# Key lengths inverted by GpSimd's power, and unit keys formed in PSUM, in the projections of a recurrence

## The chip, the core and the metric

One core of one Trainium2 chip runs the whole program. The metric is device time in microseconds (us) of one execution, as the median of several. Of the engines, PE is TensorE, DVE is VectorE, ACT is ScalarE, POOL is GpSimd and SP is SyncE.

## The reference, cut to what matters

The program is a six-part network on x of 16 x 64 x 256. The change lies in its second part, a gated recurrence, and there in what is prepared ahead of the scan:

```python
q = jax.nn.silu(x @ Wq)
k = jax.nn.silu(x @ Wk)
v = x @ Wv
log_f = jax.nn.log_sigmoid(x @ Wf1 @ Wf2)
gamma = -jax.nn.sigmoid(x @ Wgamma)
k = l2_norm(k.reshape(b, n, H, HD))      # x / maximum(norm(x), 1e-12), 16 heads of 16
a = k * gamma[..., None] * jnp.exp(gk)   # gk is log_f, so exp(gk) = f
```

The scan of a step is S = f S; sab = a S; S = S + k (sab + v); o = q S. The kernel takes two steps at a time. For that it needs, beside k, f, v and q, the coefficient of the old state in the form of a times f, and sums over a head of q times k and of a (of the next step) times k.

## The kernel before, in words

The program is a row of stages, each a block in which the five engines run their own lists in order and wait on semaphores. The order on an engine is the order of the code. The stage of the change is `recurrence_projections_stage` (named p2, lines 234 to 564). Everything in it is float32 and lies as 128 features by 512 tokens, in two halves of the tokens (`c` is 0 or 1) and two halves of the features (`m` is 0 or 1). So nearly every elementwise instruction is 128x512.

PE makes the products in the order of the list `RJOBS` into a ring of four PSUM tiles (`acc`), each of which ACT must take before it is written again: for each c the keys k0 and k1, the low-rank input `low`, and the queries; then for each c g0, f0, g1, f1 (L461: gamma and f from 16 rows of `low`); then v0 and v1, and the output gates (L466, again from 16 rows).

The lengths of the keys go through four engines. DVE squares the activated keys (L288). PE sums the squares over each head of 16 into a corner of the PSUM tiles `n_ps` (`sums`, L474). When all four sums are there, ACT takes square roots (`lengths`, L546, four instructions of 128x32), for which it loads the table of the root, and loads that of the sigmoid again behind them. DVE bounds the lengths below, inverts them and copies each 16 times (`inverse_lengths`, L292, L294, L296, into `wide`). PE turns the copies back over features by products with the identity (`spread`, L485), into `n_ps`.

Then come the unit keys and the decay vectors. POOL squares f into `k_sig` (`decays_twice`, L393). DVE multiplies gamma by the keys (L301) and by the square of f (L304), both `fadings`. DVE multiplies the keys by the inverse length in PSUM (`units`, L308) and makes `a` from gamma and the inverse length (`decays`, L313). The DVE list is: four `inverse_lengths`; then for c = 0 two `fadings`, `units` and `decays` for each m; then the same for c = 1; then `next_decays(0)` and what follows.

Behind these stand the sums by heads. POOL multiplies even queries and odd decay vectors by the even unit keys (L398, L402), PE sums them (`by_heads`, C at L493 and A at L498), and DVE adds the results into v, a and q (L321 to L347). `by_heads(1)` overwrites the PSUM tiles of `by_heads(0)`, so its C waits for `queries(0)` on DVE (L347, semaphore q_done), whose second instruction in turn waits for POOL's `faded_queries(0)` (L410). The output gates stand last on PE. ACT takes two of them, makes 12 of the 16 first value rows (L557), once v is complete, and takes the last two gates. All engines meet at the end of the block (L280), and the recurrence begins.

Of the kernel before, what the change touches and what calls it, by code (L numbers as in the profile page):

```python
# [233 lines left out]
def recurrence_projections_stage(nc, stage, X, eps, ident, xnT, W, rows, r, low, gate, own_cols, both, first_values):  # L234
# [14 lines left out]
    with Scope(nc, stage) as sc:  # L249
# [3 lines left out]
        length, inverse = (sc.sb(n, [P, 2, KD, CH, HH]) for n in ("length", "inverse"))  # L253
# [4 lines left out]
        (acc_mm, acc_read, k_done, sq_ready, n_mm, n_taken, len_ready, inv_ready, n_ready, spread_mm, unit_ready, twice_ready, part_ready, fade_ready, a_ready, q_ready, rows_ready) = (sc.sem(n) for n in (  # L258
            "acc_mm", "acc_read", "k_done", "sq_ready", "n_mm", "n_taken", "len_ready", "inv_ready", "n_ready", "spread_mm", "unit_ready", "twice_ready", "part_ready", "fade_ready", "a_ready", "q_ready", "rows_ready"))
# [20 lines left out]
        with sc.block() as block:  # L280

            @block.vector
            def _(dve):
# [6 lines left out]
                def inverse_lengths(c, m):  # L290
                    dve.wait_ge(n_taken, ONE + KD * c + m + 1)
                    nc.vector.tensor_scalar(length[:, c, m, :, :], length[:, c, m, :, :], 1e-12, None, ALU.max).then_inc(len_ready, 1)  # L292
                    dve.wait_ge(len_ready, ONE + KD * c + m + 1)
                    nc.vector.reciprocal(inverse[:, c, m, :, :], length[:, c, m, :, :]).then_inc(inv_ready, 1)  # L294
                    dve.wait_ge(inv_ready, ONE + KD * c + m + 1)
                    nc.vector.tensor_copy(wide[:, c, m, :, :, :], inverse[:, c, m, :, :].unsqueeze(3).to_broadcast([P, CH, HH, HD])).then_inc(n_ready, 1)  # L296

                def fadings(c, m):

                    wait_read(dve, c, f"g{m}")  # L300
                    nc.vector.tensor_tensor(r["gamma"][:, m, cols(c)], r["gamma"][:, m, cols(c)], r["k"][:, m, cols(c)], ALU.mult).then_inc(part_ready, 1)  # L301
                    dve.wait_ge(part_ready, ONE + KD * c + m + 1)
                    dve.wait_ge(twice_ready, ONE + KD * c + m + 1)
                    nc.vector.tensor_tensor(r["gamma"][:, m, cols(c)], r["gamma"][:, m, cols(c)], r["k_sig"][:, m, cols(c)], ALU.mult).then_inc(fade_ready, 1)  # L304

                def units(c, m):
                    dve.wait_ge(spread_mm, ONE + KD * c + m + 1)
                    nc.vector.tensor_tensor(r["k"][:, m, cols(c)], r["k"][:, m, cols(c)], n_ps[m][:, :], ALU.mult).then_inc(unit_ready, 1)  # L308

                def decays(c, m):  # L310
                    dve.wait_ge(fade_ready, ONE + KD * c + m + 1)
                    dve.wait_ge(spread_mm, ONE + KD * c + m + 1)
                    nc.vector.scalar_tensor_tensor(r["a"][:, m, cols(c)], r["gamma"][:, m, cols(c)], -1.0, n_ps[m][:, :], ALU.mult, ALU.mult).then_inc(a_ready, 1)  # L313

                def next_values(c):

                    dve.wait_ge(A_mm, ONE + c + 1)
                    dve.wait_ge(a_ready, ONE + 2 * KD)
                    for m in range(KD):
                        wait_read(dve, c, f"v{m}")  # L320
                    nc.vector.tensor_tensor(xv_ps, A_ps, steps("v", c, 0), ALU.mult).then_inc(xv_ready, 1)  # L321
                    dve.wait_ge(xv_ready, ONE + c + 1)
                    nc.vector.tensor_tensor(steps("v", c, 1), xv_ps, steps("v", c, 1), ALU.add).then_inc(v_done, 1)

                def next_decays(c):

                    dve.wait_ge(A_mm, ONE + c + 1)
                    dve.wait_ge(a_ready, ONE + 2 * KD)
                    nc.vector.tensor_tensor(xa_ps, A_ps, steps("a", c, 0), ALU.mult).then_inc(xa_ready, 1)
# [30 lines left out]
                for c in range(2):  # L360
                    for m in range(KD):
                        squares(c, m)
                for c in range(2):
                    for m in range(KD):
                        inverse_lengths(c, m)
                for c in range(2):
                    for m in range(KD):
                        fadings(c, m)
# [16 lines left out]
            def _(pool):  # L385
# [4 lines left out]
                def decays_twice(c, m):  # L390
                    pool.wait_ge(k_done, ONE + KD * c + m + 1)
                    wait_read(pool, c, f"f{m}")
                    nc.gpsimd.tensor_tensor(r["k_sig"][:, m, cols(c)], r["f"][:, m, cols(c)], r["f"][:, m, cols(c)], ALU.mult).then_inc(twice_ready, 1)  # L393
# [27 lines left out]

                for c in range(2):
                    for m in range(KD):
                        activated(c, m)
                for c in range(2):
                    for m in range(KD):
                        decays_twice(c, m)
                for c in range(2):
                    faded_twice(c)
# [7 lines left out]
                faded_queries(1)  # L437
                for c in range(2):
                    faded_keys(c)

            @block.tensor
            def _(pe):
# [34 lines left out]
                def spread(c, m):  # L477

                    pe.wait_ge(n_ready, ONE + KD * c + m + 1)
                    pe.wait_ge(n_taken, ONE + 2 * KD)  # L480
# [32 lines left out]
                for m in range(KD):  # L513
                    spread(0, m)
# [13 lines left out]
            def _(act):  # L528
# [15 lines left out]
                def lengths(c, m):  # L544
                    act.wait_ge(n_mm, ONE + 2 * KD)
                    nc.scalar.activation(length[:, c, m, :, :], n_ps[m][:, CH * HH * c:CH * HH * (c + 1)].rearrange("p (j h) -> p j h", j=CH), ACT.Sqrt).then_inc(n_taken, 1)  # L546
# [6 lines left out]
                for c, name in RJOBS:  # L553
# [7 lines left out]
                    if (c, name) == (1, "q1"):  # L561
                        for half in range(2):
                            lengths(half, 0)
                            lengths(half, 1)
# [2477 lines left out]
```

## Time and profile before

| what | value |
|---|---|
| median of 3 runs | 907.91 us (907.48 to 908.52) |
| profiled execution, first to last instruction (its span) | 905.5 us |
| what lies around the span, by the median | 2.4 us |
| PE / DVE / ACT / POOL busy | 85% / 63% / 48% / 34% |
| the stage's part that the change touches | from 199.6 to 238.7 us |

The profiled execution's own time is not given apart from its span, so the median less the span stands for what lies around it. Busy shares are averages over the whole span; in a stage of this kind another engine ends the waits. In a timeline a group of instructions is one line, with the start of the first and the time to the end of the last. Instructions of one engine overlap a little, so distances between starts are shorter than durations.

### The profile page before, as it was taken

The page shows a single profiled execution, that of the slowest core. Times are in us where ns is not written, and L with a number is a line of the kernel's source. Part 1 is how long each engine was busy: PE and PEld are TensorE (multiplying, and loading weights), DVE is VectorE, ACT ScalarE, POOL GpSimd, SP SyncE. Part 2 cuts the span into 40 slices and gives each one's busy share as a digit, 9 for nine tenths or more (in the row PEclk, how much of TensorE's full clock was granted, in tenths as well). Part 3 has the DMA queues.
Part 4 walks back from the last instruction along what each step waited for, and adds up shares of the span by engine and source line. Part 5 has one row for each costly group of instructions (what it writes and reads, how often), then busy time and mean ns, then how long its engine had stood idle before and what let it go on. Part 6 is the DMA issues. An engine that isn't in the chain of part 4 may idle for free. (4 is left out here: it accounts for less than half of the span.)

```text
span 905.5 us, 19140 instructions
## 1 busy us (share of the span) xinstructions
PE 767.5 (85%) x7000; PEld 514.0 (57%) x7000; DVE 569.9 (63%) x1297; ACT 431.1 (48%) x1284; POOL 312.1 (34%) x374
## 2 busy tenths in 40 slices
PE   5999999698899999968777399999289886867997
PEld 4788888445433333355456288887167774465334
DVE  3555555539699999977796533322587776455474
ACT  3656666462474664235365100000368883655572
POOL 2111120027477888721450441100643432233001
PEclk9899999897699999988897599999588997989899
DMA  7012530000020000000001046632545310000001
GB/s 259 18 43 52 190 107 1 2 1 1 23 71 0 1 1 1 0 1 0 2 2 48 24 149 199 186 105 82 179 146 177 107 50 2 1 3 3 0 1 49
DMA packets 44893, 51.79 MB, mean 57 GB/s; under 512 B 7072, under 2 KB 40832, under 8 KB 44544
## 3 DMA queue, kind: packets, MB, share of 16 engines
q1 hardware_dynamic: 40256, 43.48, 15.3%
q0 software_dynamic: 1536, 4.20, 1.5%
q10 hardware_dynamic: 3008, 2.88, 0.9%
q8 instruction: 57, 0.93, 0.4%
q14 instruction: 36, 0.29, 0.1%
HBM read 45.31 MB, written 5.24 MB: 56 GB/s over the span
## 5 line engine op out<-in xcount | busy, mean ns | idle before, releaser
L968 PE MATMUL r_u_ps<-r_t_in,l_same_head 128*128 128x512 f32 x124 | 69.5, 643 | 1.0
L1362 ACT ACTIVATE a_prob<-a_s_ps,a_negmax 128x256 f32<-128x256 f32 x128 | 59.1, 486 | 19.8 <-DVE a_negmax L1418 19.8
L936 POOL TENSOR_TENSOR r_q_in<-r_state,rec_q 128x512 f32<-128x512 f32 x62 | 68.0, 1097 | 0.0
L1705 ACT ACTIVATE a_prob<-a_s_ps,a_negmax 128x256 f32<-128x256 f32 x128 | 58.6, 484 | 19.3 <-DVE a_negmax L1743 19.2
L2275 PE MATMUL m_h_ps<-m_rowsT,l_w 128*128 128x256 f32 x256 | 58.8, 391 | 0.0
L1424 DVE COPY a_probT<-a_w_ps 128x512 f32<-128x512 f32 x48 | 31.5, 687 | 38.9 <-PE a_w_ps L1283 38.6
L1743 DVE TENSOR_REDUCE a_negmax<-a_s_ps 128x2 f32<-128x512 f32 x64 | 40.9, 682 | 23.0 <-PE a_s_ps L1632 23.0
L2275 PEld LDWEIGHTS m_h_ps<-m_rowsT,l_w 128*128 128x128 f32 x256 | 50.4, 197 | 7.2
L2286 PE MATMUL m_y_ps<-l_w,m_hidden 128*128 128x256 f32 x240 | 53.9, 379 | 0.0
L2321 ACT ACTIVATE m_rowsT<-m_xt_ps,l_B_s,l_B_g 128x256 f32<-128x256 f32 x16 | 8.2, 560 | 93.2 <-PE m_xt_ps L2263 93.2
L2189 DVE TENSOR_SCALAR m_hidden<-m_h_ps,l_b 128x256 f32<-128x256 f32 x64 | 28.0, 479 | 37.9 <-PE m_h_ps L2275 37.9
L926 POOL TENSOR_TENSOR r_faded<-r_state,rec_both 128x256 f32<-128x256 f32 x62 | 39.8, 641 | 33.4 <-DVE r_state L905 33.4
L1418 DVE TENSOR_REDUCE a_negmax<-a_s_ps 128x2 f32<-128x512 f32 x64 | 39.7, 683 | 17.9 <-PE a_s_ps L1274 17.9
L2286 PEld LDWEIGHTS m_y_ps<-l_w,m_hidden 128*128 128x128 f32 x240 | 45.2, 190 | 5.8
L1202 POOL TENSOR_TENSOR a_spread<-a_rden,all_half 128x256 f32<-128x256 f32 x16 | 9.8, 614 | 106.6 <-DVE a_rden L1430 106.6
L1641 PE MATMUL a_w_ps<-all_ident,a_prob 128*128 128x128 f32 x256 | 39.5, 299 | 8.3 <-ACT a_prob L1705 7.2
L896 DVE TENSOR_TENSOR r_update<-r_u_ps,rec_k 128x512 f32<-128x512 f32 x64 | 44.3, 693 | 1.6 <-PE r_u_ps L962 1.5
L892 DVE TENSOR_TENSOR r_t_in<-r_state,r_par_ps 128x512 f32<-128x512 f32 x62 | 42.6, 687 | 3.2
L1942 POOL TENSOR_TENSOR a_prob<-a_prob,a_rden 128x512 f32<-128x512 f32 x32 | 32.3, 1042 | 33.6 <-DVE a_rden L2008 33.6
L2213 POOL DMA_INDIRECT m_rows<-routed_rows,m_token x16 | 15.4, 964 | 79.8 <-PE m_xt_ps L2263 43.6
L1641 PEld LDWEIGHTS a_w_ps<-all_ident,a_prob 128*128 128x128 f32 x256 | 31.2, 154 | 17.7 <-issue 9.4
L1232 PE MATMUL a_w_ps<-a_ctxT,l_A_WkT 128*128 128x256 f32 x128 | 33.1, 404 | 7.1 <-DMA l_A_WkT<-in_A_WkT 5.9
(377 smaller groups left out, 1893.1 us busy)
## 6 DMA issues: line engine op xcount, KB each, us to landing
l_w<-in_B_w SPq DMA_DIRECT2D x16, 1024.0 KB, 5.7
a_ctxT<-in_ctxT SPq DMA_DIRECT2D x31, 256.0 KB, 2.9
a_ctx<-in_ctx SPq DMA_DIRECT2D x16, 256.0 KB, 2.8
expert_out<-m_y ACTq DMA_DIRECT2D x7, 256.0 KB, 5.6
all_X<-in_x SPq DMA_DIRECT2D x4, 256.0 KB, 5.3
l_b<-in_B_b SPq DMA_DIRECT2D x1, 1024.0 KB, 5.2
all_xnT<-own_rows SPq DMA_DIRECT2D x1, 1024.0 KB, 5.4
routed_rows<-ffn_xn SPq DMA_DIRECT2D x8, 128.0 KB, 1.8
```

Of the source, the lines that this page charges most:

```text
L892: nc.vector.tensor_tensor(t_in[m][:, :, :, :], twice(state[n % 2][m]), a, ALU.mult).then_inc(t_ready[m], 1)
L896: nc.vector.tensor_tensor(update[m][:, :, :, :], u_ps[m][:, :, :, :], steps("k", 2 * n, 2, m), ALU.mult).then_inc(upd_ready[m], 1)
L926: nc.gpsimd.tensor_tensor(faded[m][:, :, :], state[n % 2][m][:, :, :], f, ALU.mult).then_inc(faded_ready[m], 1)
L936: ins = nc.gpsimd.tensor_tensor(q_in[i % 2][m][:, :, :, :], twice(state[i % 2][m]), steps("q", 2 * i - 1, 2, m), ALU.mult)
L968: nc.tensor.matmul(u_ps[m][:, :, :, :], same_head[:, :], t_in[m][:, :, :, :], start=False, stop=True).then_inc(u_mm[m], 1)
L1362: ins = nc.scalar.activation(prob[n % 2][:, r, m, :], s_ps[r][:, m, :], ACT.Exp, bias=negmax[n % 2][:, r, m:m + 1], accum_out=den[n % 2][: ...
L1418: nc.vector.tensor_reduce(negmax[n % 2][:, r, :], s_ps[r][:, :, :], AX.X, ALU.max, negate=True).then_inc(max_ready, 1)
L1641: mm = nc.tensor.transpose(acc[:, (2 * m + c) * P:(2 * m + c + 1) * P], prob[n % 2][:, r, m, c * P:(c + 1) * P], ident[:, :])
L1705: ins = nc.scalar.activation(prob[n % 2][:, r, m, :], s_ps[r][:, m, :], ACT.Exp, bias=negmax[n % 2][:, r, m:m + 1], accum_out=den[n % 2][: ...
L1743: nc.vector.tensor_reduce(negmax[n % 2][:, r, :], s_ps[r][:, :, :], AX.X, ALU.max, negate=True).then_inc(max_ready, 1)
L2275: mm = nc.tensor.matmul(h_ps[i][:, f, :], w1[j][:, k, (2 * i + f) * P:(2 * i + f + 1) * P], rowsT[j][:, k, :], start=(k == 0), stop=(k == ...
L2286: mm = nc.tensor.matmul(y_bank(e, slice(c, c + 1))[:, 0, :], hidden[j][:, f, c * P:(c + 1) * P], w2[j][:, f, :], start=(f == 0), stop=(f = ...
```

## The change

It has six parts, all in this stage.

1. DVE bounds the sums of squares (by 1e-24) straight out of PSUM (`lengths`, two instructions of 128x64), and POOL raises them to the power -0.5 (`inverse_lengths`, two instructions of 128x64 against a tile of -0.5). ACT's four roots, DVE's four clamps of 128x32 and four reciprocals are gone. POOL does the powers between its third and its fourth activation of q.
2. ACT squares f (`decays_twice`), between its sigmoids.
3. POOL multiplies gamma by the square of f (`fadings`); the multiplication of gamma by the keys is gone.
4. DVE writes the unit keys over the inverse lengths in PSUM (`units`), makes `a` from them and gamma (`decays`), and ACT copies the unit keys to SBUF (`take_units`): c = 0 behind its last f, c = 1 behind v1 of c = 0.
5. PE spreads c = 0 between the g and f products of c = 0 and those of c = 1, before behind both.
6. POOL makes `both` (f even times f odd) behind the faded queries, before ahead of the first query sums.

```diff
+                def lengths(m):
+                    dve.wait_ge(n_mm, ONE + KD * 2)
+                    nc.vector.tensor_scalar(length[:, m, :, :, :], n_ps[m][:, 0:2 * CH * HH].rearrange("p (c j h) -> p c j h", c=2, j=CH), 1e-24, None, ALU.max).then_inc(n_taken, 1)
+                def spread_lengths(c, m):
+                    dve.wait_ge(inv_ready, ONE + m + 1)
+                    nc.vector.tensor_copy(wide[:, c, m, :, :, :], inverse[:, m, c, :, :].unsqueeze(3).to_broadcast([P, CH, HH, HD])).then_inc(n_ready, 1)
                 def units(c, m):
                     dve.wait_ge(spread_mm, ONE + KD * c + m + 1)
-                    nc.vector.tensor_tensor(r["k"][:, m, cols(c)], r["k"][:, m, cols(c)], n_ps[m][:, :], ALU.mult).then_inc(unit_ready, 1)
+                    nc.vector.tensor_tensor(n_ps[m][:, :], n_ps[m][:, :], r["k"][:, m, cols(c)], ALU.mult).then_inc(unit_mul, 1)
                 def decays(c, m):
+                    dve.wait_ge(unit_mul, ONE + KD * c + m + 1)
                     dve.wait_ge(fade_ready, ONE + KD * c + m + 1)
-                    nc.vector.scalar_tensor_tensor(r["a"][:, m, cols(c)], r["gamma"][:, m, cols(c)], -1.0, n_ps[m][:, :], ALU.mult, ALU.mult).then_inc(a_ready, 1)
+                    nc.vector.scalar_tensor_tensor(r["a"][:, m, cols(c)], n_ps[m][:, :], -1.0, r["gamma"][:, m, cols(c)], ALU.mult, ALU.mult).then_inc(a_ready, 1)
...
+                def inverse_lengths(m):
+                    pool.wait_ge(exponent_ready, ONE + 1)
+                    pool.wait_ge(n_taken, ONE + m + 1)
+                    nc.gpsimd.tensor_tensor(inverse[:, m, :, :, :], length[:, m, :, :, :], minus_half[:, :, :, :], ALU.pow).then_inc(inv_ready, 1)
+                def fadings(c, m):
+                    wait_read(pool, c, f"g{m}")
+                    pool.wait_ge(twice_ready, ONE + KD * c + m + 1)
+                    nc.gpsimd.tensor_tensor(r["gamma"][:, m, cols(c)], r["gamma"][:, m, cols(c)], r["k_sig"][:, m, cols(c)], ALU.mult).then_inc(fade_ready, 1)
...
+                def decays_twice(c, m):
+                    act.wait_ge(k_done, ONE + KD * c + m + 1)
+                    wait_read(act, c, f"f{m}")
+                    nc.scalar.activation(r["k_sig"][:, m, cols(c)], r["f"][:, m, cols(c)], ACT.Square).then_inc(twice_ready, 1)
+                def take_units(c, m):
+                    act.wait_ge(a_ready, ONE + KD * c + m + 1)
+                    nc.scalar.activation(r["k"][:, m, cols(c)], n_ps[m][:, :], ACT.Copy).then_inc(unit_ready, 1)
```

`next_values` and `next_decays` on DVE write over `n_ps` and so wait, beside what they waited for, for all four copies of the unit keys.

The rows below are the order of instructions on an engine, with no times. POOL in this stage, before (`rec_` are the tensors of the recurrence, `p_` those of the stage, `rec_k_sig` holds the square of f):

```order
L388 TENSOR_TENSOR rec_q<-rec_q,rec_q_sig 128x512 x4
L393 TENSOR_TENSOR rec_k_sig<-rec_f 128x512 x4
L420 TENSOR_TENSOR rec_both<-rec_f 128x2x256 x2
L398 TENSOR_TENSOR p_q_with_k<-rec_q,rec_k 128x512
L402 TENSOR_TENSOR p_a_with_k<-rec_a,rec_k 128x512
L406 TENSOR_TENSOR rec_a<-rec_a,rec_f 128x2x256
```

And with the change:

```order
L426 MEMSET p_minus_half 128x64
L385 TENSOR_TENSOR rec_q<-rec_q,rec_q_sig 128x512 x3
L391 TENSOR_TENSOR p_inverse<-p_length,p_minus_half 128x64 x2
L385 TENSOR_TENSOR rec_q<-rec_q,rec_q_sig 128x512
L397 TENSOR_TENSOR rec_gamma<-rec_gamma,rec_k_sig 128x512 x4
L402 TENSOR_TENSOR p_q_with_k<-rec_q,rec_k 128x512
L406 TENSOR_TENSOR p_a_with_k<-rec_a,rec_k 128x512
L410 TENSOR_TENSOR rec_a<-rec_a,rec_f 128x2x256
```

The two powers stand ahead of the fourth activation, and the four products with gamma ahead of the first product of q and k.

PE from the last sum of squares to the first sums by heads, before:

```order
L474 MATMUL p_n_ps<-l_head_of,rec_a 128x8 x4
L461 MATMUL p_acc<-rec_low,l_R_up 128x512 x8
L485 MATMUL p_n_ps<-all_ident,p_wide 128x128 x8
L454 MATMUL p_acc<-all_xnT,l_R_Wv 128x512 x2
L485 MATMUL p_n_ps<-all_ident,p_wide 128x128 x8
L454 MATMUL p_acc<-all_xnT,l_R_Wv 128x512 x2
L493 MATMUL p_x_turned<-p_q_with_k,l_same_head 128x512
```

And with the change:

```order
L482 MATMUL p_n_ps<-l_head_of,rec_a 128x8 x4
L469 MATMUL p_acc<-rec_low,l_R_up 128x512 x4
L493 MATMUL p_n_ps<-all_ident,p_wide 128x128 x8
L469 MATMUL p_acc<-rec_low,l_R_up 128x512 x4
L462 MATMUL p_acc<-all_xnT,l_R_Wv 128x512 x2
L493 MATMUL p_n_ps<-all_ident,p_wide 128x128 x8
L462 MATMUL p_acc<-all_xnT,l_R_Wv 128x512 x2
L501 MATMUL p_x_turned<-p_q_with_k,l_same_head 128x512
```

The first spread has moved ahead of the second four g and f products, which now queue behind it.

## Rows read from the trace of the kernel before

**Rows 1.** The page: granted clock of PE in 40 slices of the span.

```profile
PEclk9899999897699999988897599999588997989899
```

**Rows 2.** Windows: stretch and length in us, busy us of each engine, clock, DMA.

```profile
199.60:238.70 39.10, 31.52 (x89) 18.40 (x89) 29.77 (x46) 15.80 (x35) 23.66 (x17) 0.72 0.00 1
203.80:213.50 9.70, 9.70 (x27) 6.78 (x28) 9.53 (x14) 3.57 (x7) 7.74 (x7) 0.50 0.00 0
229.50:236.70 7.20, 7.20 (x17) 5.15 (x16) 5.50 (x11) 3.97 (x12) 1.95 (x2) 0.50 0.00 0
```

**Rows 3.** Timeline of ACT: start, us, instruction, idle before.

```profile
200.06 1.28 ACT L546 ACT_TABLE_LOAD   x1
201.83 1.28 ACT L538 ACT_TABLE_LOAD   x1
203.12 0.60 ACT L538 ACTIVATE rec_gamma<-p_acc 128x512 f32<-128x512 f32 x1
...
233.82 3.71 ACT L557 ACTIVATE all_QT<-rec_v,l_diag 128x128 f32<-128x128 f32 x12
237.34 1.09 ACT L541 ACTIVATE rec_gate<-p_acc 128x512 f32<-128x512 f32 x2
```

**Rows 4.** Timeline of PE, 199 to 237 us.

```profile
199.63 1.99 PE L461 MATMUL p_acc<-rec_low,l_R_up 16*128 16x512 f32 x8
203.77 4.27 PE L461 MATMUL p_acc<-rec_low,l_R_up 16*128 16x512 f32 x8 [2.15 <-ACT rec_gamma L538]
207.97 3.78 PE L485 MATMUL p_n_ps<-all_ident,p_wide 128*128 128x128 f32 x16
211.54 2.99 PE L454 MATMUL p_acc<-all_xnT,l_R_Wv 128*128 128x512 f32 x4
214.37 1.95 PE L485 MATMUL p_n_ps<-all_ident,p_wide 128*128 128x128 f32 x16
216.15 1.88 PE L454 MATMUL p_acc<-all_xnT,l_R_Wv 128*128 128x512 f32 x4
217.87 1.02 PE L493 MATMUL p_x_turned<-p_q_with_k,l_same_head 128*128 128x512 f32 x2
218.73 1.02 PE L498 MATMUL p_x_turned<-p_a_with_k,l_same_head 128*128 128x512 f32 x2
219.59 3.60 PE L454 MATMUL p_acc<-all_xnT,l_R_Wv 128*128 128x512 f32 x8
226.62 1.26 PE L493 MATMUL p_x_turned<-p_q_with_k,l_same_head 128*128 128x512 f32 x2 [3.43 <-DVE rec_q L347]
229.51 7.19 PE L466 MATMUL p_acc<-l_R_up,rec_low 16*128 16x256 f32 x16
```

**Rows 5.** Timeline of DVE.

```profile
202.18 0.43 DVE L296 COPY p_wide<-p_inverse 128x512 f32<-128x512 f32 x1
...
205.85 0.82 DVE L296 COPY p_wide<-p_inverse 128x512 f32<-128x512 f32 x1
...
214.78 1.88 DVE L304 TENSOR_TENSOR rec_gamma<-rec_gamma,rec_k_sig 128x512 f32<-128x512 f32 x1
...
221.78 0.70 DVE L329 TENSOR_TENSOR p_n_ps<-p_x_turned,rec_a 128x512 f32<-128x512 f32 x1
...
225.78 0.69 DVE L347 TENSOR_TENSOR rec_q<-p_x_turned,rec_q 128x512 f32<-128x512 f32 x1
```

**Rows 6.** Groups by line, POOL and DVE: busy us, mean ns, idle before.

```profile
L936 POOL TENSOR_TENSOR r_q_in<-r_state,rec_q 128x512 f32<-128x512 f32 x62 | 68.0, 1097 | 0.0
L926 POOL TENSOR_TENSOR r_faded<-r_state,rec_both 128x256 f32<-128x256 f32 x62 | 39.8, 641 | 33.4 <-DVE r_state L905 33.4
L388 POOL TENSOR_TENSOR rec_q<-rec_q,rec_q_sig 128x512 f32<-128x512 f32 x4 | 5.1, 1265 | 30.6 <-ACT rec_q_sig L538 30.6
L398 POOL TENSOR_TENSOR p_q_with_k<-rec_q,rec_k 128x512 f32<-128x512 f32 x2 | 3.0, 1504 | 3.3 <-DVE rec_k L308 3.2
...
L304 DVE TENSOR_TENSOR rec_gamma<-rec_gamma,rec_k_sig 128x512 f32<-128x512 f32 x4 | 5.4, 1347 | 0.1
```

More of the change, by code:

```diff
@@ L252, in recurrence_projections_stage @@
         n_ps = [sc.ps(f"n_ps{j}", [P, N]) for j in range(KD)]
-        length, inverse = (sc.sb(n, [P, 2, KD, CH, HH]) for n in ("length", "inverse"))
+        length, inverse = (sc.sb(n, [P, KD, 2, CH, HH]) for n in ("length", "inverse"))
+        minus_half = sc.sb("minus_half", [P, 2, CH, HH])
         wide = sc.sb("wide", [P, 2, KD, CH, HH, HD])
@@ L288, in squares @@
                     nc.vector.tensor_tensor(r["a"][:, m, cols(c)], r["k"][:, m, cols(c)], r["k"][:, m, cols(c)], ALU.mult).then_inc(sq_ready, 1)
[L290 to L304, printed above, removed]
+                def lengths(m):
+                    dve.wait_ge(n_mm, ONE + KD * 2)
+                    nc.vector.tensor_scalar(length[:, m, :, :, :], n_ps[m][:, 0:2 * CH * HH].rearrange("p (c j h) -> p c j h", c=2, j=CH), 1e-24, None, ALU.max).then_inc(n_taken, 1)
@@ L362, in _ @@
                         squares(c, m)
+                for m in range(KD):
+                    lengths(m)
                 for c in range(2):
                     for m in range(KD):
-                        inverse_lengths(c, m)
+                        spread_lengths(c, m)
                 for c in range(2):
-                    for m in range(KD):
-                        fadings(c, m)
                     for m in range(KD):
@@ L420, in faded_twice @@
                     nc.gpsimd.tensor_tensor(both[:, :, c * N // 2:(c + 1) * N // 2], steps("f", c, 0), steps("f", c, 1), ALU.mult).then_inc(both_faded, 1)
+                nc.gpsimd.memset(minus_half[:, :, :, :], -0.5).then_inc(exponent_ready, 1)
+                activated(0, 0)
+                activated(0, 1)
+                activated(1, 0)
+                for m in range(KD):
+                    inverse_lengths(m)
+                activated(1, 1)
                 for c in range(2):
                     for m in range(KD):
[L424 to L429, printed above, removed]
+                        fadings(c, m)
                 queries_with_keys(0)
@@ L437, in _ @@
                 faded_queries(1)
+                for c in range(2):
+                    faded_twice(c)
                 for c in range(2):
@@ L512, in _ @@
                         product(c, name)
-                for m in range(KD):
-                    spread(0, m)
+                    if c == 0:
+                        for m in range(KD):
+                            spread(0, m)
                 product(0, "v0")
@@ L560, in _ @@
                         normed.take(act, 4 + ("k0", "k1", "low", "q0").index(name))
[L561 to L564, printed above, removed]
+                    if name == "g1":
+                        decays_twice(c, 0)
+                    if name == "f1":
+                        decays_twice(c, 1)
+                    if (c, name) == (1, "f1"):
+                        take_units(0, 0)
+                        take_units(0, 1)
+                    if (c, name) == (0, "v1"):
+                        take_units(1, 0)
+                        take_units(1, 1)
 def gated_output_stage(nc, stage, history, own, ident, gate, gated, gain, Wo, X, eps):
```

16 lines of the change are left out of this document (5 added, 11 removed).

## The prediction, blind

> **What bounds the kernel now.** I read the page first. PE is busy for most of the span, but that is an average over stages, and its clock dips in single slices [rows 1]. So I read the stage of the change by itself. Of its 39.1 us from the first g product to the start of the recurrence, PE shows 31.5 us busy at a mean granted clock of 0.72 [rows 2]: neither PE nor any other engine is full. DMA moves nothing. What ends the stage has to be followed wait by wait.
>
> From the end backwards: ACT ends last, at 238.4 us, with two gates of 1.09 us behind twelve value rows of 3.71 us [rows 3]. These waited for the second gate from PE, whose four gate products begin at 229.51 and take 7.19 us at half clock [rows 2, 4]. Ahead of them PE stood idle for 3.43 us, up to 226.62, for DVE's `queries(0)` (L347), which ended at 226.47 [rows 4, 5]. PE had offered the sums for DVE's chain of seven instructions (L329 to L347) at 219.6, but DVE reached the first only at 221.78 [rows 4, 5]. DVE was late for two reasons. Its inversion began only after ACT's table load of 1.28 us [rows 3], and its eight `fadings` instructions run slowly: L304 takes 1.35 us on average and up to 1.88, where L329, which has one operand in PSUM, takes 0.70 [rows 5, 6]. Both operands of L304 lie in SBUF, where POOL is at work at the same time, so I put it down to the two engines waiting for each other there.
>
> The front of the stage has its own stall: ACT is held by two table loads with the roots between them from 200.06 to 203.12 [rows 3], PE's ring is full, PE is idle for 2.15 us, and from 203.77 it runs at half clock, the lower of its two levels (1.2 against 2.4 GHz), for 9.7 us [rows 2, 4].
>
> **The change, part by part.** All times are those of the profiled execution, whose span is 905.5 us; the median is 2.4 us above the span, and I move both by the same amount.
>
> *ACT's front.* The two table loads and the roots go: 203.12 less 200.06 is 3.1 us, which ACT gets back [rows 3]. It gets four squares and four copies of 128x512, at 0.55 us each (two gates in 1.09) 4.4 us in all. ACT is busy 15.8 of 39.1 us [rows 2, 3], so this is covered; only the place of a copy matters, below.
>
> *The powers.* The last sum of squares is there at about 199.6 [rows 4], DVE's two clamps of 64 columns take an estimated 0.2 us each (a copy of 512 takes 0.43 [rows 5]), and POOL's first power starts near 200.0 and the second behind it. No row shows a power on POOL. Let X be its time for 128x64. From below: POOL's product costs 0.641 us for 256 columns and 1.097 for 512 [rows 6], so 1.78 ns a column, and 64 columns cost 0.3 us. From above, a power is a chain of arithmetic on each column (a logarithm, a product, an exponential). I choose its length: 12 passes at 1.78 ns give 64 x 12 x 1.78 = 1.4, with 0.2 us of start about X = 1.6 to 1.7; 40 passes give 4.8 us, my upper bound. I take **X = 1.7**, which is nearer to the row of the product, the one operation of this form that the trace has, than to the upper bound, and I keep 0.3 and 4.8 for the range.
>
> *DVE's copies.* A copy into `wide` takes 0.43 us alone and 0.82 beside POOL [rows 5]: it was held until POOL's instruction ended. So I let the first copy start not at the end of the first power but at the end of the second, 200.0 + 2 X = 203.4, and the first spread can start at 203.85. If the copy could run beside the power instead, the first spread would start at about 202.2 and the sum would be up to 1.6 us better; the row speaks against that.
>
> *PE's middle.* From 201.5 to 203.85 PE is idle, as long as before, so I keep half clock behind it. Then: two spreads 3.6, the second four g and f products 3.8 (between twice their full-clock time, 3.4, and the 4.2 of before), v0 2.8, two spreads 1.8, v1 1.7, the two sums by heads 1.7 [rows 4]. That ends at 219.3. Before, it was 219.6. The gain of 3.1 us at the front is thus nearly all spent on the powers and the idle time ahead of the spread. Moving the spread ahead costs nothing, since g and f for c = 1 are wanted later.
>
> *DVE and POOL behind it.* DVE loses its 8 `fadings` instructions, the slow ones, and the reciprocals. The four products with gamma go to POOL, at 1.27 us each [rows 6], and end near 213, before `a` of c = 1 is wanted. The copies of the unit keys for c = 1 stand on ACT behind v1 of c = 0: PE ends v1 at 217.7, ACT takes it by 218.3, and the two copies behind it end near 219.3. So DVE starts its chain when PE's sums are there, at 219.5 and not 221.78: **2.3 us** earlier. Its last instruction waits for POOL's `faded_queries(0)`: three POOL products of 1.50 us [rows 6] behind the last unit key give 219.3 + 4.5 = 223.8. The chain would have been ready at 223.5. So `queries(0)` ends at 224.6, and **1.9 us** are left of the 2.3. `both`, moved behind these, has cover: POOL ends near 230 to 232, ahead of ACT.
>
> *The last stretch.* PE's wait before the second sums shrinks from 3.43 us to about 1.9. In before, the clock fell in these sums, and the gates ran at half: the sums took 2.9 us (226.62 to 229.51) and the first two gates 3.5 of the 7.19. At full clock the same work takes 1.7 and 1.7 us (L493 and L498 start 0.86 us apart there [rows 4]), 3.0 less. Before, a stall of 2.15 us was followed by half clock, and one of 3.43 too; 1.9 us has no row. I take 2.3 of the 3.0. Behind the second gate, 3.6 for value rows and 1.1 for gates remain as they are.
>
> **Sum:** -1.9 - 2.3 = **-4.2 us**, that is 907.9 - 4.2 = 903.7 us. The end moves by about 2 us for each us of X, since both powers stand ahead of the first copy.
>
> **The rivals.** *A. The power is nearly as cheap as a product (X of 0.3 to 0.8).* Then the first spread starts 2 to 2.8 us earlier, PE's idle time is under 1 us, and part of the 3.9 us that half clock costs in spreads and g and f products goes too. At X = 0.3: -4.2 - 2.8 - 2.4 = -9.4, so 898.5 us. For it: the memory side of 64 columns is tiny. Against: a power is no single pass.
>
> *B. The power takes what it frees (X near 4).* At X = 3.8 the sum is -4.2 + 2 x 2.1 = 0, about 908 us. ACT's 3.1 us then only became POOL's wait. For it: each step of the chain may wait for the one before. No row of before shows such a chain.
>
> *C. Slower: POOL becomes the bound of the stage.* The mechanism is one: the power, at the head of POOL's in-order list, holds the fourth activation, the four products with gamma and all that DVE and PE do behind it. It decides from X = 4.7 on, where the sum passes +1.8. At X = 6, +8.6 - 4.2 = +4.4, or 912 us. A first call that has to fetch code would do the same: once Y us ahead of the first power move the end by Y, and above 6 us they make it slower. The Trainium skill (GPSIMD Engine Reference, section Instruction dispatch) states a load of about 6 us for the first call of a freshly loaded function; with that the sum would be +1.8. Against it: on POOL's list no instruction is added besides the product form with another operation.
>
> *D. The clock stays low in the last stretch.* Then only -1.9 us, 906.0 us. It lies inside the forecast's own range.
>
> **How the numbers follow.** About 0.2% (1.8 us) is what a measurement of this kernel can tell from no change. The forecast (X from 0.8 to 2.9, with D in it) has a chance of 0.44 and 901 to 906 us; A 0.20; B (X of 2.9 to 4.7) 0.18; C 0.18. Faster by over 0.2% is the forecast and A: 0.64. The range takes in X = 0.3 at the low end (898.5) and X = 4.8 at the high end (-4.2 + 6.2 = +2.0, so 910): it leaves out C but for its edge.
>
> **What would show it.** In the profile after: no table load between 199 and 204 us; two powers on POOL with their length X, right behind 200.0; the first copy into `wide` starting or ending only behind the second power; PE idle from 201.5 to about 203.9; L329's like on DVE (now L326) at 219.5 with the wait ended by PE or ACT, not by DVE's own work; `queries(0)` ended by POOL's faded queries; ACT's last gate at 234.2 against 238.4. Wrong would be: X over 3 us; PE at full clock through the first spreads (better than said); a `take_units` copy or a POOL product with gamma on which DVE waits for over 1 us beyond this schedule; or a recurrence stage whose own length differs by more than 1 us.

## The result, and the profile after

The change makes the kernel slower: 923.91 us (923.09 to 924.91) against 908.21 us, a ratio of 1.0172 with a 95% interval of 1.0156 to 1.0188. The forecast was 903.7 us, and the range ended at 910.0. The loss is 15.7 us.

The whole of it lies in the stage of the change. From the first product of g to the first product of the recurrence, before took 238.74 - 199.63 = 39.1 us [rows 2, 4], the second time by this line:

```profile
238.74 5.46 PE L962 MATMUL r_u_ps<-all_QT,l_same_head 128*128 128x512 f32 x6 [2.04 <-PEq L280]
```

After, by PE's timeline (start, us, instruction, idle before and what ended it):

```profile
199.04 1.99 PE L469 MATMUL p_acc<-rec_low,l_R_up 16*128 16x512 f32 x8
210.75 2.08 PE L493 MATMUL p_n_ps<-all_ident,p_wide 128*128 128x128 f32 x8 [9.72 <-DVE p_wide L298]
222.21 2.08 PE L493 MATMUL p_n_ps<-all_ident,p_wide 128*128 128x128 f32 x8 [9.38 <-DVE p_wide L298]
224.21 3.79 PE L469 MATMUL p_acc<-rec_low,l_R_up 16*128 16x512 f32 x8
...
236.77 1.02 PE L506 MATMUL p_x_turned<-p_a_with_k,l_same_head 128*128 128x512 f32 x2
...
243.21 1.64 PE L501 MATMUL p_x_turned<-p_q_with_k,l_same_head 128*128 128x512 f32 x2 [1.98 <-DVE rec_q L344]
...
254.19 4.35 PE L982 MATMUL r_u_ps<-all_QT,l_same_head 128*128 128x512 f32 x6 [3.73 <-PEq L281]
```

It is 254.19 - 199.04 = 55.2 us, 16.0 more. PE has no table load to wait for, and still stands idle for 9.72 and 9.38 us ahead of the two first spreads; in before it had one wait of 2.15 us here, ahead of the second g and f products [rows 4]. Each time it waits for a copy into `wide` on DVE. DVE in turn waits for POOL (its lines stand in the last section), whose timeline is this:

```profile
199.52 21.12 POOL L391 TENSOR_TENSOR p_inverse<-p_length,p_minus_half 128x64 f32<-128x64 f32 x2 [1.35 <-DVE p_length L294]
220.61 1.25 POOL L385 TENSOR_TENSOR rec_q<-rec_q,rec_q_sig 128x512 f32<-128x512 f32 x1
```

Two powers of 64 columns fill 21.1 us, 10.57 each. The view of the tile `p_inverse` gives the shortest, the median and the longest in nanoseconds:

```profile
L391 POOL TENSOR_TENSOR p_inverse<-p_length,p_minus_half x2: 10544/10566/10589, 199.5 to 210.1; 128x64 f32<-128x64 f32 x2
```

I had taken 1.7 us for each, and 4.8 us as the upper bound. Behind the powers the order of the waits is the foreseen one, with a lower clock than I had. From the second of the two spreads (222.21) to the recurrence it takes 32.0 us. The forecast had 30.7 us (203.85 to 238.74 - 4.2), with both spreads in them. v0 and the spreads of c = 1 took 3.78 and 2.85 us, at a granted clock of 0.53 from 222.2 to 234.0, and I had written 2.8 and 1.8.

### The profile page after: what moved, and what is told of

Read it like the earlier page. It is cut to its first block and busy times, and to the rows that moved or that the text cites. A ratio compares the mean times of both kernels' runs of the same rounds, so it can differ in the third digit from the quotient of the medians.

```text
span 921.5 us, 19133 instructions
## 1 busy us (share of the span) xinstructions
PE 765.9 (83%) x7000; PEld 511.0 (55%) x7000; DVE 560.5 (61%) x1283; ACT 433.1 (47%) x1286; POOL 333.3 (36%) x377
## 5 line engine op out<-in xcount | busy, mean ns | idle before, releaser
L1382 ACT ACTIVATE a_prob<-a_s_ps,a_negmax 128x256 f32<-128x256 f32 x128 | 59.2, 486 | 19.5 <-DVE a_negmax L1438 19.5
```

The source lines that it names most:

```text
L1382: ins = nc.scalar.activation(prob[n % 2][:, r, m, :], s_ps[r][:, m, :], ACT.Exp, bias=negmax[n % 2][:, r, m:m + 1], accum_out=den[n % 2][: ...
```

## The experiments

Twelve kernels ran. Three of them leave the inverse lengths out and are there for their time alone: `exponent_one`, `product` and `product_x16`. The stage's length is taken from one profiled execution each, from the first g product to the first product of the recurrence; the ratio is that of the whole program, against executions of before made beside it.

| run | stage, us | less before | ratio, 95% interval |
|---|---|---|---|
| before | 39.1 | | |
| the change | 55.2 | +16.0 | 1.0172 (1.0156 to 1.0188) |
| product | 31.8 | -7.3 | 0.9915 (0.9890 to 0.9941) |
| product_x16 | 35.3 | -3.8 | 0.9951 (0.9931 to 0.9971) |
| quarters | 49.0 | +9.9 | one execution |
| exponent_one | 55.3 | +16.2 | one execution |
| power_alone | 60.0 | +20.9 | 1.0253 (1.0228 to 1.0278) |
| roots | 35.1 | -4.0 | 0.9967 (0.9948 to 0.9985) |
| fadings_dve | 35.4 | -3.7 | 0.9954 (0.9931 to 0.9977) |
| old_units | 36.1 | -3.0 | 0.9979 (0.9956 to 1.0002) |
| reordered | 33.5 | -5.6 | 0.9925 (0.9902 to 0.9947) |
| newton3 | 35.8 | -3.3 | 0.9945 (0.9920 to 0.9969) |
| newton2 | 37.1 | -2.0 | 0.9966 (0.9938 to 0.9994) |
| gates_early | 36.3 | -2.8 | 0.9985 (0.9957 to 1.0013) |

Before itself spread over 906 to 914 us in these executions, so differences of 2 us in the whole program are at the edge of what they tell. Part of the spread comes from elsewhere. Behind the first product of the recurrence the profiled execution took 666.1 to 667.7 us in ten of the fourteen kernels, before and the change among them, and 670.0 to 670.8 us in `quarters`, `power_alone`, `roots` and `old_units`. In three of the four the difference comes up some 430 us later, in an attention stage that none of the edits touches, and in `power_alone` mostly in a later one; why is not known. So the stage and the whole can differ by 3 to 4 us for one kernel.

### What a power costs

**Fewer columns in each power.** Four powers of 128x32, in the order of the halves c.

```diff
-                    nc.gpsimd.tensor_tensor(inverse[:, m, :, :, :], length[:, m, :, :, :], minus_half[:, :, :, :], ALU.pow).then_inc(inv_ready, 1)
+                    nc.gpsimd.tensor_tensor(inverse[:, m, c, :, :], length[:, m, c, :, :], minus_half[:, c, :, :], ALU.pow).then_inc(inv_ready, 1)
```

> The change with four powers of 128x32 in place of two of 128x64. If a power's time goes by its columns (165 ns each): 5.3 us each, and the last copy starts at the same time as in the change; time within 2 us of it. If it is a fixed time for each instruction (code fetched or a call set up anew each time): 10.5 us each, 42 us in all, and some 20 us longer.

The view of the tile, in nanoseconds (shortest, median, longest):

```profile
L391 POOL TENSOR_TENSOR p_inverse<-p_length,p_minus_half x4: 5416/5419/5467, 200.5 to 216.8; 128x32 f32<-128x32 f32 x4
```

5.42 us for 32 columns and 10.57 for 64: (10.57 - 5.42) / 32 = 0.161 us a column, and 0.27 us beside them, which is what a product of this size costs in all. So the time goes by columns. The stage was 6.1 us shorter than the change's, which I had not expected: both halves m of c = 0 are inverted after 11 us and not after 21. It was not more, since DVE's list has the unit keys behind the fourth copy, and PE then waited 5.13 us for ACT's copies of them. The one time measured was 921.73 us, 2.2 us below the change. The stage also began 1.0 us later in this execution, and what lies behind it took 670.7 us against 667.3, so of the 6.1 us 1.7 are left in the span.

**Other data.** An exponent of 1.0.

```diff
-                nc.gpsimd.memset(minus_half[:, :, :, :], -0.5).then_inc(exponent_ready, 1)
+                nc.gpsimd.memset(minus_half[:, :, :, :], 1.0).then_inc(exponent_ready, 1)
```

> The change with 1.0 in place of -0.5 as the exponent, so that the lengths are not inverted. If the time of a power goes by its data (a general path for roots, a short one for whole numbers): well under 10.5 us each. If not: 10.5 us each and the time of the change, 924 us.

```profile
L391 POOL TENSOR_TENSOR p_inverse<-p_length,p_minus_half x2: 10544/10567/10590, 200.3 to 210.8; 128x64 f32<-128x64 f32 x2
```

The same to a nanosecond, and 924.43 us. No short path for an easy exponent shows.

**No power, its place kept short.** A product stands in the place of each power.

```diff
-                    nc.gpsimd.tensor_tensor(inverse[:, m, :, :, :], length[:, m, :, :, :], minus_half[:, :, :, :], ALU.pow).then_inc(inv_ready, 1)
+                    nc.gpsimd.tensor_tensor(inverse[:, m, :, :, :], length[:, m, :, :, :], minus_half[:, :, :, :], ALU.mult).then_inc(inv_ready, 1)
```

> The change with both powers replaced by products of the same shape (128x64), so that the inverse lengths are left out and the unit keys are wrong by a factor. Theory 1 (the time of the power on POOL is the whole loss, and the rest of the change gains what the blind sum gave it at X = 0.3): 898.5 us, 9.4 below before. Theory 2 (the end moves by 2 us for each us of X from the measured end of the change, since both powers stand ahead of nearly everything): 923.9 - 2 x (10.57 - 0.3) = 903.4 us, 4.5 below before. Theory 3 (the other five parts cost about what they free): 907 to 909 us.

901.43 us, 7.2 below before (908.67). That lies between theories 1 and 2 and rules out the third: all that is not the powers is a gain, taken together. PE's timeline has three lines for the rest:

```profile
202.68 2.07 PE L493 MATMUL p_n_ps<-all_ident,p_wide 128*128 128x128 f32 x16
...
220.74 1.10 PE L501 MATMUL p_x_turned<-p_q_with_k,l_same_head 128*128 128x512 f32 x2 [1.98 <-DVE rec_q L344]
...
223.38 7.19 PE L474 MATMUL p_acc<-l_R_up,rec_low 16*128 16x256 f32 x16
```

PE goes without idle time into the first spread, which now runs at full clock (2.07 us for 16, against 3.78 [rows 4]). But the wait ahead of the second sums is still 1.98 us, and the gates behind it take 7.19 us, as in before. That is nearly all that my -9.4 had too much: up to the second sums the run is 7.0 us ahead of before (220.74 - 200.77 against 226.62 - 199.63), where the sum for X = 0.3 had 1.9 + 2.8 + 2.4 = 7.1. The last stretch then gave 0.3 us, and I had taken 2.3.

**The power's place held for 1.6 us.**

```diff
+                    pool.wait_ge(q_ready, ONE + 1)
+                    nc.gpsimd.tensor_tensor(both[:, m, :], r["q"][:, 0, 0:N], r["q_sig"][:, 0, 0:N], ALU.mult)
+                    nc.gpsimd.tensor_tensor(inverse[:, m, :, :, :], length[:, m, :, :, :], minus_half[:, :, :, :], ALU.mult).then_inc(inv_ready, 1)
```

> The change with each power replaced by two products, one of 128x512 (1.27 us) into a tile that is written later anyway and one of 128x64 (0.3 us), so that the place of the power is held for some 1.6 us and the inverse lengths are left out. Theory 1 (my blind sum was right but for X, and 2 us go with each us of X): 903.7 us by the blind sum, 901.4 + 2 x 1.3 = 904.0 us from the run with products. Rival (below some length the powers lie beside ACT's first sigmoids and cost nothing, since PE's queue has other work): 901 to 902 us.

904.88 us against 909.19, a ratio of 0.9951, so 4.5 us less (3.8 in the stage). The blind sum with an X of this size was -4.2. So the sum held for its X, but two errors in it nearly cancel, which is luck. Up to the second sums the run is 1.0 us ahead of before (225.62 - 199.67 against 226.62 - 199.63), and I had 1.9; behind them it gains 2.8 more, and I had 2.3. The first copy did not wait for the second stand-in. It started beside that one's product of 128x512 and took 1.48 us, and PE idled 1.59 and 0.53 us and not 2.3:

```profile
201.71 1.48 DVE L298 COPY p_wide<-p_inverse 128x512 f32<-128x512 f32 x1 [1.57 <-POOL p_inverse L393]
203.40 4.30 DVE L298 COPY p_wide<-p_inverse 128x512 f32<-128x512 f32 x3 [0.21 <-POOL p_inverse L393]
```

Between this run and the change X differs by 9.0 us and the stage by 19.9, so the end moves by 2.2 us for each us of X. I had said about 2.

**The powers alone in the kernel before.** Parts 2 to 6 of the change are undone.

```diff
-                        activated(c, m)
+                nc.gpsimd.memset(minus_half[:, :, :, :], -0.5).then_inc(len_ready, 1)
+                activated(0, 0)
+                activated(0, 1)
+                activated(1, 0)
+                for m in range(KD):
+                    powers(m)
+                activated(1, 1)
```

> The kernel before with part 1 of the change alone (clamps out of PSUM on DVE, powers on POOL, no roots and no reciprocals). Theory 1: 21.1 us of powers against 3.1 us of roots and loads on ACT; DVE's fadings and POOL's squares of f stand behind the powers, so 908.7 + 18 = 926 to 928 us, 2 to 4 above the change. Rival (the other parts cost something that the power hides in the change): below 923 us.

931.63 us, a ratio of 1.0253: worse than I expected and 7.7 us above the change. 4.9 us of that lie in the stage (60.0 against 55.2), and 2.7 behind it, where the edits do not reach (670.0 against 667.3). POOL's and DVE's timelines show what comes behind the powers:

```profile
222.19 5.02 POOL L401 TENSOR_TENSOR rec_k_sig<-rec_f 128x512 f32<-128x512 f32 x4
227.17 2.93 POOL L428 TENSOR_TENSOR rec_both<-rec_f 128x512 f32<-128x512 f32 x2
```

```profile
226.34 1.41 DVE L305 TENSOR_TENSOR rec_gamma<-rec_gamma,rec_k_sig 128x512 f32<-128x512 f32 x1
...
234.66 1.87 DVE L305 TENSOR_TENSOR rec_gamma<-rec_gamma,rec_k_sig 128x512 f32<-128x512 f32 x1
236.46 1.98 DVE L302 TENSOR_TENSOR rec_gamma<-rec_gamma,rec_k 128x512 f32<-128x512 f32 x1
```

The squares of f queue behind the powers on POOL, and then run beside DVE's slow products. So parts 2 to 6 are worth 4.9 us of the stage behind the powers. With roots they are worth 4.0 (next run); from one execution each, the two can't be told apart with certainty.

### What the other parts are worth

**Roots on ACT again.** The change with ACT's roots and DVE's clamps and reciprocals in place of the powers.

```diff
-                    nc.gpsimd.tensor_tensor(inverse[:, m, :, :, :], length[:, m, :, :, :], minus_half[:, :, :, :], ALU.pow).then_inc(inv_ready, 1)
+                    nc.scalar.activation(length[:, m, :, :, :], n_ps[m][:, 0:2 * CH * HH].rearrange("p (c j h) -> p c j h", c=2, j=CH), ACT.Sqrt).then_inc(n_taken, 1)
...
+                    nc.vector.tensor_scalar(length[:, m, :, :, :], length[:, m, :, :, :], 1e-12, None, ALU.max).then_inc(len_ready, 1)
+                    nc.vector.reciprocal(inverse[:, m, :, :, :], length[:, m, :, :, :]).then_inc(inv_ready, 1)
```

> The change without the powers: ACT takes square roots (two of 128x64, two table loads around them) and DVE clamps and inverts (two of each), as before, with the other five parts of the change as they are. Theory 1 (the power alone is the loss; fadings off DVE and the unit keys in PSUM gain): the unit chain on DVE starts about 2 us earlier than before, 903 to 905 us. Theory 3 (the other parts gain nothing): 907 to 909 us.

906.01 us, a ratio of 0.9967 (0.9948 to 0.9985): faster than before, by 3.0 us in the ratio (1.4 to 4.7) and 4.0 in the stage. The stage's gain lies in the 3.7 to 5.7 that I expected, the whole a little below them. The chain on DVE behind the first sums by heads starts 18.0 us behind the first g product (218.90, from the line below, less 200.92), and not 22.2 (221.78 - 199.63, [rows 4, 5]). Its start now waits for PE and no longer for DVE's own work, as the blind text said:

```profile
218.90 0.70 DVE L326 TENSOR_TENSOR p_n_ps<-p_x_turned,rec_a 128x512 f32<-128x512 f32 x1 [1.57 <-PE p_x_turned L497]
...
223.44 0.69 DVE L344 TENSOR_TENSOR rec_q<-p_x_turned,rec_q 128x512 f32<-128x512 f32 x1 [0.58 <-POOL rec_q L408]
```

**The products with gamma on DVE.** In the run with roots, `fadings` moves from POOL to DVE, ahead of the unit keys of each half.

```diff
-                    nc.gpsimd.tensor_tensor(r["gamma"][:, m, cols(c)], r["gamma"][:, m, cols(c)], r["k_sig"][:, m, cols(c)], ALU.mult).then_inc(fade_ready, 1)
+                    nc.vector.tensor_tensor(r["gamma"][:, m, cols(c)], r["gamma"][:, m, cols(c)], r["k_sig"][:, m, cols(c)], ALU.mult).then_inc(fade_ready, 1)
```

> The run with roots, with the four products of gamma and the square of f back on DVE, ahead of the unit keys of each half. If it was POOL's taking them that gains: DVE's instructions beside POOL take 1.4 to 1.9 us again and come ahead of the decay vectors; 1 to 2 us above the run with roots (906.0). If it was leaving out the other product (gamma times the keys) and the order: the same as the run with roots.

904.28 us, a ratio of 0.9954, and 35.4 us in the stage against 35.1; the intervals of the two ratios overlap for the most part. In this schedule POOL is idle while DVE multiplies, and the four instructions take 0.69 us each. So it isn't POOL's taking them that gains.

**Parts 2, 5 and 6 alone.** The kernel before with squares of f on ACT, the first spread early and `both` late; unit keys, roots and all eight products of DVE stay.

```diff
-                    nc.gpsimd.tensor_tensor(r["k_sig"][:, m, cols(c)], r["f"][:, m, cols(c)], r["f"][:, m, cols(c)], ALU.mult).then_inc(twice_ready, 1)
+                    nc.scalar.activation(r["k_sig"][:, m, cols(c)], r["f"][:, m, cols(c)], ACT.Square).then_inc(twice_ready, 1)
```

> The kernel before with parts 2, 5 and 6 of the change alone: ACT squares f, the first spread stands ahead of the second g and f products, both is made late. Roots, unit keys in SBUF and the product of gamma and the keys stay as before. If the gain of the run with roots (0.33% below before, 4.0 us in the stage) comes from taking POOL's work out of the way of DVE's products: most of it is here too, 905 to 907 us, and the eight fadings instructions take 0.7 us. If it comes from leaving out the four products of gamma and the keys: 908 to 909 us, no gain.

907.08 us, a ratio of 0.9979 (0.9956 to 1.0002), which neither shows nor excludes a gain. The trace says more. The products of c = 0 now take 0.69 us, three of the four of c = 1 still meet POOL's products with the unit keys and with f:

```profile
207.29 0.69 DVE L304 TENSOR_TENSOR rec_gamma<-rec_gamma,rec_k_sig 128x512 f32<-128x512 f32 x1
...
213.34 1.87 DVE L304 TENSOR_TENSOR rec_gamma<-rec_gamma,rec_k_sig 128x512 f32<-128x512 f32 x1
215.12 1.98 DVE L301 TENSOR_TENSOR rec_gamma<-rec_gamma,rec_k 128x512 f32<-128x512 f32 x1
```

DVE's chain starts 220.32 - 200.87 = 19.5 us behind the first g product: 2.7 of the 4.2 us that the run with roots wins there. The other 1.5 go with the unit keys in PSUM and the product left out, which no run takes apart. At the end of the stage 3.0 of 4.0 us are left: PE starts the second sums 24.3 us behind the first g product, against 23.4 in the run with roots and 27.0 in before.

### A version that beats both, and attempts at more

**Three moves in the run with roots.**

```diff
-                    if (c, name) == (1, "f1"):
+                    if (c, name) == (1, "f0"):
                         take_units(0, 0)
                         take_units(0, 1)
...
                 faded_decays(0)
+                faded_queries(0)
                 queries_with_keys(1)
                 decays_with_keys(1)
-                faded_queries(0)
...
+                for name in ("gate0", "gate1"):
+                    product(0, name)
                 by_heads(1)
-                for c in range(2):
-                    for name in ("gate0", "gate1"):
-                        product(c, name)
+                for name in ("gate0", "gate1"):
+                    product(1, name)
```

> The run with roots and three moves. ACT copies the unit keys of c = 0 behind f0 of c = 1, not behind its last square (PE waited 1.30 us for them). POOL's faded queries of c = 0 stand ahead of the second query sums (DVE waited 0.58 us). PE makes the two gates of c = 0 in the 1.98 us in which it waited for the second sums. Each us is on the chain that ends the stage: 1.3 + 0.6 + 2 to 3, so 901 to 902 us. If the waits only change their names (squares of f late for POOL instead): 904 to 906 us.

901.23 us, a ratio of 0.9925 (0.9902 to 0.9947), as expected: 6.8 us below before and so 22.5 below the change. In PE's timeline the waits ahead of the second spreads and of the second sums are gone, and the gates run at full clock:

```profile
222.50 1.99 PE L465 MATMUL p_acc<-l_R_up,rec_low 16*128 16x256 f32 x8
224.41 1.12 PE L492 MATMUL p_x_turned<-p_q_with_k,l_same_head 128*128 128x512 f32 x2
225.38 1.02 PE L497 MATMUL p_x_turned<-p_a_with_k,l_same_head 128*128 128x512 f32 x2
226.33 1.99 PE L465 MATMUL p_acc<-l_R_up,rec_low 16*128 16x256 f32 x8
```

But the stage is only 1.7 us shorter than with roots (33.5 against 35.1), and I had added up 3.9 to 4.9. PE no longer waited for the unit keys, and then made the second g and f products and v0 at half clock, in 3.79 and 3.78 us against 2.10 and 1.98. So DVE's chain starts 19.8 us behind the first g product (219.17 - 199.37), and not 18.0; what the stage gains, it gains behind that. The agreement of the whole is in part luck: behind the stage this execution took 666.6 us, the one with roots 670.8.

**The third move alone, in the kernel before.** The gates of c = 0 ahead of the second sums.

```diff
+                for name in ("gate0", "gate1"):
+                    product(0, name)
                 by_heads(1)
```

> The kernel before with one move: PE makes the two gates of c = 0 ahead of the second sums by heads, in the 3.43 us in which it waited for them. Theory 1 (the end of the stage is gates behind sums behind DVE): ACT's value rows start when v is complete, at 231.1, and not behind the second gate at 233.8, so 2.5 us less or more (PE's clock may stay up): 904 to 906.5 us against 909. Rival (ACT's end is set elsewhere): no difference.

907.04 us, a ratio of 0.9985 (0.9957 to 1.0013). The stage of the profiled execution is 2.8 us shorter, as expected, but the whole doesn't show it clear of its interval. It stays open what this move is worth by itself.

**No roots at all.** DVE makes the inverse root by an integer seed and Newton steps, in the reordered run.

```diff
+                    chain.link(nc.vector.tensor_scalar(t.bitcast(I32), x.bitcast(I32), 1, None, ALU.arith_shift_right))
+                    chain.link(nc.vector.tensor_scalar(y.bitcast(I32), t.bitcast(I32), -1.0, float(0x5f3759df), ALU.mult, ALU.add))
+                    for i in range(3):
+                        chain.link(nc.vector.tensor_tensor(t, y, y, ALU.mult))
+                        chain.link(nc.vector.scalar_tensor_tensor(t, t, -0.5, x, ALU.mult, ALU.mult))
+                        chain.link(nc.vector.scalar_tensor_tensor(y, t, 1.5, y, ALU.add, ALU.mult))
```

> The reordered run without square roots: DVE makes the inverse root by itself (an integer shift and difference for the seed, three Newton steps, 13 small instructions in all, 128x128 or less). Theory 1 (ACT's two table loads and roots, 3 us ahead of the first sigmoid of gamma, are on the path wherever an equally short inversion exists): at 0.2 us an instruction the first copy starts 2.6 us behind the clamp, about as early as with roots, and ACT is free 3 us earlier; 899 to 901 us, 0.5 to 2 us below the reordered run (901.2). Rival (PE is bound by the copies into wide, and ACT's time at the front is cover): the same as the reordered run, 901 to 902 us.

> The same with two Newton steps. Three instructions less ahead of the first copy, 0.6 us earlier; since the end moves by up to 2 us for each us only where both halves wait, here 0.3 to 0.8 us below the run with three steps. Rival: no difference, if PE's half clock ends the stretch.

Both were wrong: 904.49 and 905.15 us, and 35.8 and 37.1 us in the stage against 33.5 of the reordered run. The ratios alone would not tell the three apart. DVE's timeline with three steps shows the size that I had wrong:

```profile
200.43 1.20 DVE L297 TENSOR_SCALAR p_spare<-p_length 128x128 int32<-128x128 int32 x1
...
202.91 0.29 DVE L300 TENSOR_TENSOR p_spare<-p_inverse 128x128 f32<-128x128 f32 x1
203.23 1.38 DVE L301 SCALAR_TENSOR_TENSOR p_spare<-p_spare,p_length 128x128 f32<-128x128 f32 x1
204.65 1.23 DVE L303 SCALAR_TENSOR_TENSOR p_inverse<-p_spare,p_inverse 128x128 f32<-128x128 f32 x1
...
206.96 1.43 DVE L309 COPY p_wide<-p_inverse 128x512 f32<-128x512 f32 x4
```

An instruction of the chain costs 0.33 us and not 0.2, and three of them fell beside POOL's activation and its two products with gamma, and took 1.2 to 1.4 us. The first copy starts 7.2 us behind the first g product (206.96 - 199.81), against 3.3 with roots (202.67 - 199.37 in the reordered run). ACT's table loads were not worth so much. With two steps the first spread does start 1.0 us earlier (6.6 us behind the first g product against 7.6), but PE's granted clock stays at 0.50 from 206.9 to 217.9, where with three steps it is 1.00 from 210.9 to 217.0. So the rival of that run, PE's half clock, had the mechanism:

```profile
206.91 3.78 PE L493 MATMUL p_n_ps<-all_ident,p_wide 128*128 128x128 f32 x16 [4.60 <-DVE p_wide L309]
210.62 3.78 PE L470 MATMUL p_acc<-rec_low,l_R_up 16*128 16x512 f32 x8
214.34 3.78 PE L463 MATMUL p_acc<-all_xnT,l_R_Wv 128*128 128x512 f32 x4
```

## Why the prediction was wrong

**The step that failed is the term X.** "From above, a power is a chain of arithmetic on each column"; I chose 12 passes at the price of a product's column and 40 as the bound. Measured: 10.57 us for 128x64, 0.161 us a column. At the product's 1.78 ns a column [rows 6] that is 90 passes. The first end of the bound was read from a row, the other end was a number of passes that I chose, and no row bore it. An upper bound of 4.8 us for an operation with no row in the trace was no bound, and with a slope of 2 us for each us of X the range had to depend on it.

**The estimate from the Trainium skill was nearer, and still 2.5 times too low.** Its rule for a dependent float32 step (GPSIMD Engine Reference, section Performance pitfalls for Q7 kernels) gave an estimate of 4.3 us with the 20 steps that I assumed; the measured column would be about 48 such steps. No run here tests the rule; the number of steps was mine.

**Rival C had the mechanism and the sign.** The power at the head of POOL's in-order list held DVE's copies and PE's spreads. The second g and f products stand behind the first spreads on PE, so ACT in turn waited 22.8 us for a product. Rival C was given 0.18 and a price for X = 6. With X = 10.57 its own rule, -4.2 + 2 x 8.87, gives +13.5 us; +15.7 was measured, and the slope between the runs is 2.2.

```profile
226.32 0.60 ACT L547 ACTIVATE rec_gamma<-p_acc 128x512 f32<-128x512 f32 x1 [22.83 <-PE p_acc L469]
```

The variant with code fetched on a first call is excluded: the two powers took 10.544 and 10.589 us. The Trainium skill (GPSIMD Engine Reference, section Instruction dispatch) tells of some 6 us for the first call of a freshly loaded function; no such time shows here.

**The rest of the sum was right in sum, in part by luck.** At X of about 1.6, -4.2 was forecast and a ratio of 0.9951 (-4.5 us, -3.8 in the stage) measured, with two errors that nearly cancel (the run with the place of the power held). The terms:

- *ACT's front, 3.1 us:* the table loads are gone, but the gain is 2.3 us. ACT takes the first g 1.2 us behind the product's start and not 3.5 (203.12 - 199.63 [rows 3, 4]), and waits 0.76 us of that for PE.
- *DVE's copies wait for the second power:* wrong, and with it the reason given for the 2 us for each us of X, that both powers stand ahead of the first copy. A copy started right behind the first power and took 0.55 us beside the second one (below). It changed little, since DVE's second copy, and with it the other half of the first spread, needs the second power anyway. That is where the slope comes from.
- *DVE's chain starts when PE's sums are there:* right in the change and in `roots`, `fadings_dve`, `reordered`, `product` and `product_x16` (1.57 to 1.61 us of waiting for PE).
- *`queries(0)` waits for POOL's faded queries, 0.4 us:* right, 0.58 us in the change (0.86 at X = 1.6).
- *PE's wait ahead of the second sums shrinks to 1.9 us:* 1.98 measured, and 2.26 at X = 1.6. What the clock does behind it is not settled by the wait's length: after 1.98 us the gates took 7.19 us in the product run (granted clock 0.50) and 3.98 in the change (0.93, the line below), and after 5.31 us in `old_units` 4.13 (0.89). I had taken 2.3 of 3.0 us for it; the last stretch gave 0.3 in the product run, 1.1 in the change and 2.8 at X = 1.6.

```profile
246.48 3.98 PE L474 MATMUL p_acc<-l_R_up,rec_low 16*128 16x256 f32 x16
```

**The forecast of A (-9.4 at X = 0.3)** was 2 us too good, by the last stretch at half clock.

## What to carry to other kernels

An operation that stands in no row of the trace has no upper bound from the rows of another operation. If the time moves by twice its cost, measure it first with one small kernel, or let the range reach to where its cost is absurd. Here a power of 128x64 took 35 times as long as a product of the same shape on the same engine, so two table loads with the roots between them, 3.1 us, were the better bargain. And where an edit has several parts, the bad one hides the good ones: undoing the powers alone turned +15.7 us into -3.0, and three moves read off the remaining waits made it -6.8 (in the stage +16.0, -4.0 and -5.6).

## What the runs showed of the hardware

- GpSimd's tensor-tensor power took 0.161 us a column and 0.27 us beside it, for 32 and 64 columns of 128 partitions, with exponents of -0.5 and of 1.0 alike. Two products of the same shape took 0.60 us together (`product`).
- A DVE copy into `wide` that started 0.05 us behind a power took 0.55 us (0.47 and 0.48 in `quarters`), and one that started 0.06 us behind a POOL product of 128x512 took 1.48 us. Alone it took 0.43 [rows 5]. So a power did not hold back a copy at its start as a product does. All copies that met a power did so at its start; what a power does to DVE later on, no run shows. The copies in the change:

```profile
210.14 0.55 DVE L298 COPY p_wide<-p_inverse 128x512 f32<-128x512 f32 x1 [10.64 <-POOL p_inverse L391]
220.67 4.29 DVE L298 COPY p_wide<-p_inverse 128x512 f32<-128x512 f32 x3 [9.98 <-POOL p_inverse L391]
```

- The first copy stands beside the second power. The three copies of the second line stand beside POOL's activation and products with gamma, and take 4.29 us together; in the run with roots, where POOL was idle, all four took 1.36. The Trainium skill (SBUF — State Buffer, section Who interferes with whom) calls the ports to SBUF that DVE and GpSimd share an exclusive lock, held for the whole instruction of whichever issues first. The products agree with it, with copies of 1.48 us; the power doesn't, 0.55 us against the 10.5 us that the copy would have had to wait, unless it takes the ports only some time after its start, which no run tests.
